# The weighted sums of graph layer 3: transposed one-hots of a whole group by one VectorE compare, one-hots on ScalarE, picks and scores a group ahead

## The reference

```
ft = (feat @ W.T).reshape(n, 4, 64)
a1 = einsum('nhd,hd->nh', ft, attn_l);  a2 = einsum('nhd,hd->nh', ft, attn_r)
e  = leaky_relu(a1[src] + a2[dst], 0.2)
m  = segment_max(e, dst)
ex = exp(e - m[dst])
s  = segment_sum(ex, dst)
out = elu(segment_sum(ft[src] * (ex / s[dst]), dst))
```

## Time and profile before

| | us |
|---|---|
| three runs | 6770.54, 6778.85, 6797.03 |
| span of the profiled execution | 6776.8 |
| of it the stage `L3Max` | 5426 to 6074 |
| of it the stage `L3Sum` | 6074 to 6476 |
| first and last exponential of `L3Sum` (51 groups apart) | 6085.5 and 6468.1 |

### The profile page before, as it was taken

The page is one execution under the profiler, slowest core; times in us unless marked ns, Lnnn a source line. Parts: engine busy times, 40 slices in busy tenths (PEclk is TensorE's granted clock), DMA queues, the critical chain, the costliest instruction groups (busy, mean ns, idle before and its releaser), DMA issues. The chain is left out here.

```text
span 6776.8 us, 96400 instructions
## 1 busy us (share of the span) xinstructions
PE 4712.7 (70%) x22485; PEld 3146.3 (46%) x22485; DVE 3844.5 (57%) x15258; ACT 2230.7 (33%) x8279; POOL 3457.0 (51%) x3739
## 2 busy tenths in 40 slices
PE   4566675748885555638667774888778478878858
PEld 3223333637772222424356663666567233336635
DVE  8676543120016666351567777777532667778876
ACT  0000001202232222302355554444323188874421
POOL 3646665546636666456555553555112166656610
PEclk9786656869995776855799997999879699989978
DMA  1133335546745666013154444777456156564410
GB/s 47 50 97 92 92 92 172 178 140 225 233 138 158 179 181 170 4 49 102 48 149 125 126 125 140 209 208 207 137 145 176 45 169 173 172 155 140 141 44 20
DMA packets 510322, 889.51 MB, mean 131 GB/s; under 512 B 97783, under 2 KB 380358, under 8 KB 501334
## 3 DMA queue, kind: packets, MB, share of 16 engines
q0 software_dynamic: 170800, 477.14, 25.9%
q1 hardware_dynamic: 278544, 277.57, 13.1%
q10 hardware_dynamic: 60438, 128.64, 6.1%
HBM read 711.86 MB, written 171.14 MB: 130 GB/s over the span
## 5 line engine op out<-in xcount | busy, mean ns | idle before, releaser
L998 PE MATMUL bank<-small 128*125 128x256 f32 x1660 | 760.6, 583 | 475.7 <-DVE small L965 269.5
L946 POOL DMA_INDIRECT small<-tabA,idxD x830 | 803.9, 969 | 449.0 <-issue 189.2
L998 PEld LDWEIGHTS bank<-small 128*125 128x125 f32 x1660 | 359.9, 265 | 875.7 <-issue 457.0
L977 DVE TENSOR_TENSOR big<-big,bank 125x256 f32 x830 | 347.6, 419 | 492.0 <-PE bank L998 308.1
L2467 POOL DMA_INDIRECT small<-tabC,idxD x415 | 394.2, 950 | 342.3 <-issue 123.2
L2509 ACT ACTIVATE small<-cst,small 128x128 f32<-128x128 f32 x1660 | 532.3, 388 | 95.8 <-issue 42.0
L2520 PE MATMUL bank<-small 128*125 128x512 f32 x830 | 474.2, 655 | 125.8 <-issue 97.5
L2221 POOL DMA_INDIRECT big<-tabB,idxD x415 | 392.1, 945 | 321.2 <-PE bank L2287 199.5
L1341 DVE COPY small<-bank 128x256 f32<-128x256 f32 x176 | 74.6, 425 | 832.3 <-PE bank L1381 405.5
L2026 POOL DMA_INDIRECT small<-tabT,idxS x415 | 392.3, 945 | 297.5 <-PE bank L1988 180.7
L780 POOL DMA_INDIRECT recs<-pkS,rowS x391 | 383.4, 981 | 256.1 <-issue 101.0
(11 more groups left out here) (460 smaller groups left out, 11594.9 us busy)
## 6 DMA issues: line engine op xcount, KB each, us to landing
small<-eaS SPq DMA_DIRECT2D x830, 128.0 KB
big<-in_L_w ACTq DMA_DIRECT2D x56, 1024.0 KB
eaS<-small SPq DMA_DIRECT2D x415, 128.0 KB
big<-in_L2f_w ACTq DMA_DIRECT2D x64, 512.0 KB
ytab<-small ACTq DMA_DIRECT2D x176, 128.0 KB
small<-tabA,idxD POOLq DMA_INDIRECT x830
idxS<-in_ea SPq DMA_DIRECT2D x78, 128.0 KB
locS<-in_ea SPq DMA_DIRECT2D x78, 128.0 KB
```

Source lines behind the costliest of these rows:

```text
L946: g.indirect_dma_start(out=self.gb[k % self.RG], out_offset=None, in_=K.tabA, in_offset=row_index(K.idxD, k)).then_inc(*self.got.up(k))
L977: v.tensor_tensor(rows, rows, K.bank[k % 4][0:PT, 0:D], ALU.add).then_inc(*self.added.up)
L998: p.matmul(self.K.bank[k % 4][0:PT, 0:D], self.oh[k % self.RO][:, 0:PT], self.gb[k % self.RG], start=True, stop=True).then_inc(*self.summe ...
```

## The change

Before `L3Max`'s own work, `LocRows` turns the table of local numbers: four transpositions on TensorE, four copies on ScalarE into bf16 rows, one DMA to the new DRAM table `rowsD`, and SP waits for it. `Flipped` then makes, in `L3Sum`, the 8 transposed one-hots of a group at once: SP reads 8 rows of `rowsD` into all 128 partitions (1024 bf16 each), and VectorE compares them with the partition's own number (`lane`). The transposition and the copy per tile are gone. The three parts are added by one reduction over PSUM. The one-hots are made on ScalarE, as relu(1 - (iota - loc)^2), two instructions, the second waiting for the first. Picks of group g+1 stand before the first product of group g, its scores after the third add of group g, its exponential after the sixth one-hot of group g. `RO` becomes 8, `RG` 16, and 6 PSUM banks hold products.

```diff
+class LocRows:
+    NB, P = 4, 104
+    def tensor(self, p):
+        for b in range(self.NB):
+            for c, (loc, table) in enumerate(self.pieces):
+                m = p.transpose(K.bank[4 + b][0:self.P, 128 * c:128 * c + 128], loc[:, self.P * b:self.P * (b + 1)], K.ident)
+        m.then_inc(*self.flipped.up)
+    def scalar(self, a):
+        a.wait_ge(*self.flipped.n(1))
+        for b in range(self.NB):
+            a.activation(self.row[0:self.P, w * b:w * (b + 1)], K.bank[4 + b][0:self.P, 0:w], ACT.Copy).then_inc(*self.turned.up)
+    def sync(self, s):
+        s.wait_ge(*self.turned.all)
+            s.dma_start(table.rearrange("(b p) e -> p b e", p=self.P), rows[:, :, c, :]).then_inc(*self.kept.up)
+        s.wait_ge(*self.kept.all)
+class Flipped:
+    G = 8
+    def sync(self, s, g):
+        if g >= 2:
+            s.wait_ge(*self.made.n(g - 1))
+        row = self.table[g * self.G:(g + 1) * self.G, :].rearrange("k e -> (k e)")
+        s.dma_start(self.row[g % 2], row.unsqueeze(0).broadcast_to([128, self.G * 128])).then_inc(*self.row_in.up(g))
+    def vector(self, v, g):
+        v.wait_ge(*self.row_in.n(g))
+        v.tensor_scalar(self.ohT[g % 2], self.row[g % 2], self.K.lane[:, 0:1], None, ALU.is_equal).then_inc(*self.made.up)
 class L3Max:
+        self.locs.sync(s)      # first in sync(); likewise locs.scalar(a), locs.tensor(p)
 class L3Sum:
-    GB, RO, RG = 8, 18, 8
+    GB, RO, RG, RS = 8, 8, 16, 6
     def sync(self, s):
+        self.flip.sync(s, 0)
+        self.flip.sync(s, 1)
         for k in range(NTE):
             if k >= self.RG:
                 s.wait_ge(*self.summed.n(k - self.RG + 1))
             s.dma_start(self.gb[k % self.RG][:, 0:D], K.eaS[k * 128:(k + 1) * 128, :]).then_inc(*self.got.up(k))
+            if k % self.GB == 0 and k // self.GB + 2 < self.n_g:
+                self.flip.sync(s, k // self.GB + 2)
+    def scores(self, v, gi):
+        v.wait_ge(*self.picked.n(gi + 1))
+        v.tensor_reduce(bv, b3, AXX, ALU.add).then_inc(*self.taken.up)
+        ...                                  # the four operations of lines 2609 to 2615
     def vector(self, v):
+        for k in range(NTE):
+            gi, j = k // self.GB, k % self.GB
+            if j == 1 and gi + 2 < self.n_g:
+                v.wait_ge(*self.picked.n(gi + 1))
+                flip.vector(v, gi + 2)
+            if j == 3 and gi + 1 < self.n_g:
+                self.scores(v, gi + 1)
+            rows = pr.acc[0:PT, bass.ds(at.at(k), AW)]
+            v.wait_ge(*self.summed.n(k + 1))
+            if k:
+                v.wait_ge(*self.added.n(k))
+            v.tensor_tensor(rows, rows, K.bank[2 + k % self.RS][0:PT, 0:AW], ALU.add).then_inc(*self.added.up)
+    def one_hot(self, a, k):
+        if k >= self.RO:
+            a.wait_ge(*self.summed.n(k - self.RO + 1))
+        a.activation(self.sq[k % 2], self.K.iota, ACT.Square, bias=self.negD[:, k:k + 1]).then_inc(*own.up)
+        a.wait_ge(*own.all)
+        a.activation(self.oh[k % self.RO], self.sq[k % 2], ACT.Relu, scale=-1.0, bias=self.K.ones[:, 0:1]).then_inc(*self.oneh.up)
     def scalar(self, a):
+        self.powers(a, 0)
+        for k in range(NTE):
+            self.one_hot(a, k)
+            if j == 5 and gi + 1 < self.n_g:
+                self.powers(a, gi + 1)       # waits for score(gi + 1), then Exp
+            if j == 0:
+                a.wait_ge(*self.expo.n(gi + 1))
+            if k >= self.RG:
+                a.wait_ge(*self.summed.n(k - self.RG + 1))
+            a.activation(self.gb[k % self.RG][:, D:AW], pr.EX[:, 4 * k:4 * k + 4], ACT.Copy).then_inc(*self.joined.up)
+    def pick(self, p, at, gi):
+        p.wait_ge(*self.flip.ready(gi * self.GB))
+        if gi >= 2:
+            p.wait_ge(*self.taken.n(gi - 1))
+        for j, k in enumerate(self.tiles(gi)):
+            m = p.matmul(K.bank[gi % 2][:, 24 * j:24 * j + 24], self.flip.at(k)[0:PT, :], pr.am3[0:PT, bass.ds(at.at(k), 24)], start=True, stop=True)
+        m.then_inc(*self.picked.up)
     def tensor(self, p):
+        self.pick(p, at, 0)
+        for k in range(NTE):
+            if k % self.GB == 0 and gi + 1 < self.n_g:
+                self.pick(p, at, gi + 1)
+            ...                              # waits for oneh, weighted, joined and added(k - 6), then the product
```

More of the change, by code:

```diff
@@ L1989, in split_sum, with __init__, at, ready @@
     return m
+class LocRows:
+    NB, P = 4, 104
+    def __init__(self, K, al, pieces):
+        self.K, self.pieces, self.n = K, pieces, len(pieces)
+        self.row = al(self.NB * self.n * 64, BF16)
+        self.flipped, self.turned, self.kept = K.mark(1), K.mark(self.NB), K.dma(self.n)
+    def tensor(self, p):
+        K = self.K
+        for b in range(self.NB):
[3 more added lines that the diff above has]
+    def scalar(self, a):
+        K, w = self.K, 128 * self.n
+        a.wait_ge(*self.flipped.n(1))
+        for b in range(self.NB):
+            a.activation(self.row[0:self.P, w * b:w * (b + 1)], K.bank[4 + b][0:self.P, 0:w], ACT.Copy).then_inc(*self.turned.up)
+    def sync(self, s):
+        rows = self.row[0:self.P, :].rearrange("p (b c e) -> p b c e", b=self.NB, c=self.n)
+        s.wait_ge(*self.turned.all)
+        for c, (loc, table) in enumerate(self.pieces):
+            s.dma_start(table.rearrange("(b p) e -> p b e", p=self.P), rows[:, :, c, :]).then_inc(*self.kept.up)
+        s.wait_ge(*self.kept.all)
+class Flipped:
+    G = 8
+    def __init__(self, K, table, al):
+        self.K, self.table = K, table
+        self.n_g = EP // self.G
+        self.row = [al(self.G * 64, BF16) for _ in range(2)]
+        self.ohT = [al(self.G * 64, BF16) for _ in range(2)]
+        self.row_in, self.made = K.ring(2, self.n_g), K.mark(self.n_g)
+    def sync(self, s, g):
[6 more added lines that the diff above has]
+        v.tensor_scalar(self.ohT[g % 2], self.row[g % 2], self.K.lane[:, 0:1], None, ALU.is_equal).then_inc(*self.made.up)
+    def at(self, k):
+        return self.ohT[k // self.G % 2][:, k % self.G * 128:(k % self.G + 1) * 128]
+    def ready(self, k):
+        return self.made.n(k // self.G + 1)
 class L2Max:
@@ L2457, in __init__ @@
         self.gb = [g(AW) for _ in range(self.RG)]
+        self.locs = LocRows(K, K.W, ((K.locD, K.rowsD),))
         self.got, self.kept_rows = K.ring(self.RG, NTE, "gather"), K.ring(self.RG, NTE)
@@ L2502, in scalar @@
         K, pr = self.K, self.pr
+        self.locs.scalar(a)
         for k in range(NTE):
@@ L2513, in tensor @@
         K, pr = self.K, self.pr
+        self.locs.tensor(p)
         for k in range(NTE):
@@ L2581, in gpsimd @@
             g.tensor_tensor(rows, rows, self.pr.EX[:, 4 * k:4 * k + 4].unsqueeze(2).broadcast_to([128, 4, 64]), ALU.mult).then_inc(*self.weighted.up)
+    def scores(self, v, gi):
+        K, pr, own = self.K, self.pr, self.K.own_v
+        c0, n = gi * self.GB, len(self.tiles(gi))
+        b3 = K.bank[gi % 2][:, 0:24 * n].rearrange("p (k c h) -> p k h c", c=3, h=8)
+        bv = self.ame[gi % 2][:, 0:8 * n].rearrange("p (k h) -> p k h", h=8)
+        A1v = pr.A1[:, 4 * c0:4 * (c0 + n)].rearrange("p (k h) -> p k h", h=4)
+        q = self.am4[gi % 2][:, 0:4 * n]
+        qv = q.rearrange("p (k h) -> p k h", h=4)
+        v.wait_ge(*self.picked.n(gi + 1))
+        v.tensor_reduce(bv, b3, AXX, ALU.add).then_inc(*self.taken.up)
+        v.wait_ge(*self.taken.n(gi + 1))
+        if gi >= 2:
+            v.wait_ge(*self.expo.n(gi - 1))
+        v.tensor_tensor(qv, A1v, bv[:, :, 0:4], ALU.add).then_inc(*own.up)
+        v.wait_ge(*own.all)
+        v.scalar_tensor_tensor(out=q, in0=q, scalar=0.2, in1=q, op0=ALU.mult, op1=ALU.max).then_inc(*own.up)
+        v.wait_ge(*own.all)
+        v.tensor_tensor(qv, qv, bv[:, :, 4:8], ALU.subtract).then_inc(*own.up)
+        v.wait_ge(*own.all)
+        v.tensor_scalar(q, q, 0.0, None, ALU.min).then_inc(*self.score.up)
@@ L2623, in vector @@
[L2623 to L2643 removed]
+        flip.vector(v, 0)
@@ new lines, in vector @@
+        flip.vector(v, 1)
+        self.scores(v, 0)
+        for k in range(NTE):
[10 more added lines that the diff above has]
+            v.tensor_tensor(rows, rows, K.bank[2 + k % self.RS][0:PT, 0:AW], ALU.add).then_inc(*self.added.up)
@@ new lines, in vector, with powers @@
+        v.wait_ge(*self.added.all)
+    def one_hot(self, a, k):
+        if k >= self.RO:
+            a.wait_ge(*self.summed.n(k - self.RO + 1))
+        own = self.K.own_a
+        a.activation(self.sq[k % 2], self.K.iota, ACT.Square, bias=self.negD[:, k:k + 1]).then_inc(*own.up)
+        a.wait_ge(*own.all)
+        a.activation(self.oh[k % self.RO], self.sq[k % 2], ACT.Relu, scale=-1.0, bias=self.K.ones[:, 0:1]).then_inc(*self.oneh.up)
+    def powers(self, a, gi):
+        t = self.tiles(gi)
+        a.wait_ge(*self.score.n(gi + 1))
+        a.activation(self.pr.EX[:, 4 * t[0]:4 * t[-1] + 4], self.am4[gi % 2][:, 0:4 * len(t)], ACT.Exp).then_inc(*self.expo.up)
```

113 lines of the change are left out of this document (27 added, 86 removed).

## The result

The changed kernel takes 6834.82 us (median of 4 runs, 6827.31 to 6842.22), the kernel before, in four runs (the three above and one more), 6785.74. The ratio is 1.0072, 95% interval 1.0052 to 1.0091: slower, by 49 us. A second comparison, on a chip on which the kernel before takes 5981.15 us, gave 6030.82, ratio 1.0086 [1.0067, 1.0105]. The other stages are faster there; `L3Sum` is not. The forecast was 6805, the range 6757 to 6842.

A forecast was written before the change was run, and what follows sets the result against it. VectorE set the old 7.50 us beat; the changed round trip averages 7.6, plus 0.33 for the clock and 0.07 for stretched compares, 8.0 us per group: +26 us, 6805 on the median, range 6757 to 6842.

The forecast's parts named there:

- The forecast's case: In `L3Sum`, a period between 7.5 and 8.6 us per group of 8 tiles, 6779 to 6835 us; chance 0.48.
- ScalarE: In `L3Sum`, ScalarE's work takes 0.88 us a tile and 7.17 a group, a floor under the period.
- The last product of the group before: On TensorE, it starts at 0.05 us, when its one-hot is ready, and keeps TensorE for 0.51.
- Picks: On TensorE, eight picks before product 0 take 0.80 us; product 0 starts at 1.36 instead of 0.92.
- Load of offsets: On TensorE, ahead of every second block of picks: costs 1.1 to 1.2 us, covers the product's 0.51; period 7.95.
- Compare: On VectorE, the compare of 1024 16-bit columns takes 0.43 us, from 2.60 to 3.03, ahead of the second add.
- Rival C: In `L3Sum`, the compare meets GpSimd's multiplications and is 0.47 us late in every group: +50 us, 6829; chance 0.12.
- Clock: TensorE's granted clock in `L3Sum` is 0.87, a quarter of the time at 1.2 GHz, costing 0.33 us per group.
- Sum: Over `L3Sum`'s 51 intervals, 8.0 us against 7.50 gives 25.5, plus 0.5, less 0.2 for the tail: +26 us.
- A: In `L3Sum`, buffers hide VectorE's and TensorE's delays and ScalarE's 7.17 us sets the beat: -15 us, 6763; chance 0.20.
- B: In `L3Sum`, TensorE's lower clock holds all through, period 8.9 us: +71 us, 6850; chance 0.12.
- D: In `L3Sum`, ScalarE takes some 0.6 us a tile and VectorE's work sets 6.8: -36 us, 6743; chance 0.08.

## Why the prediction was right, and where not

The time fell into the range, near its upper end and 30 us above the number given; 7 of the 30 are the kernel before, whose fourth run raised its median, 23 are the change. The forecast's case occurred, in its upper part: the period of 8.33 is above the 8.17 from which a difference can be told, so the outcome is slower, which had 0.39, and not within 0.5%, which had 0.53. The mechanism was right in the main: every second period is longer, the exponential waits for the last score in all 52 groups, and the clock costs what was said. Sizes were off, all in the round trip, and one limit was overlooked.

*ScalarE.* 0.82 us per tile, not 0.88. The relu follows 0.42 after the square, not 0.49: its wait for ScalarE's own result costs 0.03 where the earlier trace rows showed 0.10. By its own words the prediction would be wrong in this term, and was, but towards a lower floor (6.8 instead of 7.17), which the loop never let show. From the exponential to the next group's first square go 1.88, not 1.99. With the loop cut ScalarE is the floor (the version with load early and exponential late).

*The last product of the group before.* I let it start when its one-hot was ready, at 0.05. It also waits for the small copy behind the relu, and starts at 0.31. Put ahead of the one-hot, the copy gave 0.21 per group back.

*Picks.* 0.80 forecast, 1.06 from the first pick to product 0 (6309.60 to 6310.66). The product ahead of them is in their way for 0.32 only, not 0.51. Together product 0 starts at 1.69, not 1.36. The exponential comes at 5.54 instead of 5.27, and the period is 7.42 instead of 7.26.

*Load of offsets, the step that failed most.* I let it begin with the last product and end 1.2 later, picks at 1.25. It takes 1.11, but it stands behind both weight loads of that product, so the first pick comes 1.51 after the product and not 1.20. A group with a load is 0.65 longer than forecast at full clock, 8.60 for 7.95: 0.26 by the copy, 0.31 by the load, 0.29 by the picks behind it, less 0.21 in small terms (0.84 instead of 0.90 from product 0 to its add, where by the earlier trace rows I should have added 0.92, and ScalarE's shorter tiles). On the mean that is 0.33, nearly the whole error. That the load mattered at all was right, and its early version shows it: without it at the group's edge the change costs nothing.

*Compare.* 0.43 forecast, 0.48 measured. Rival C did not decide the time, but the reason given against it is only half right. GpSimd's multiplications do end about as the compare starts, but in a group without a load slightly later: the compare is held to 5.26 after the exponential in 12 of 49 groups and lasts 0.51 to 0.55 there, under 0.02 per group on the mean where I had put 0.07. What the prediction doesn't have is that this makes a limit of its own, 7.42, right behind the loop that I added up. The runs with early picks, with the small copy ahead and, in part, with the exponential late ran into it; there its price was up to 0.50 (0.98 long), and 0.36 with the one-hots on VectorE, where I had 0.47.

*Clock.* 0.87 and 0.33 per group forecast, 0.87 and 0.33 measured. The agreement is luck: I took a clock between those of other stages and put it to the missing transpositions. The run with the load early has these missing too and a clock of 0.99. It is the load at the group's edge that lets it fall, so both costs have one cause.

*Sum.* 7.6 + 0.33 + 0.07 = 8.0 forecast, 8.0 + 0.33 = 8.33 measured. Of the 0.33 missed, 0.33 lie in the groups with a load and 0.08 in the others, and the 0.07 for stretched compares did not come. 51 x 0.33 = 17 of the 23 us missed on the profiled execution. The tail was 1.4 us longer, not 0.2 shorter, since its products wait for one-hots 0.82 apart, and 4.3 came from other stages. `LocRows` cost nothing: from the first gather to the last reduction `L3Max` takes 646.5 us in both kernels. A, B and D did not occur. The early load comes near A's number (7.42), but not to its cause, since the exponential still waits in all 52 groups.

## What to carry to other kernels

When a change turns two independent streams into a loop over three engines, add up the loop at its joints: what each engine has queued ahead of and behind the waiting instruction, small copies included. Add up a second loop for each engine that the same result sets off, and see what runs at the same time as it: here GpSimd's multiplications, which hold up a compare that has nothing to do with them. Several runs that end at one and the same period (7.42) are the sign of such a limit. A load of offsets belongs into the slack of a group, not at its edge, and an instruction that waits for a far result behind all that others need now. Both are moves of a line, and took this change from 0.9% slower to 0.6% faster than before.

## What the runs showed of the hardware

- A load of 16 offsets takes 1.11 us in TensorE's queue and 1.10 in VectorE's (26 of each in the changed kernel). On TensorE it starts behind both weight loads of the product ahead of it, 0.25 after that product's start, and the next weight load comes 1.51 after it; the product's multiplication runs on beside the load (until 6165.97, the load being at 6165.5). On VectorE the load puts 0.75 us between two adds.
- One such load per 16 tiles, at the edge of a group, goes with a granted clock of 0.87 in the stage, and of 0.99 when it is moved into slack; the slow stretch can fall into the next group (0.78, behind a group at 1.00). Such a load is not the only thing that does this: with the one-hots on VectorE the stage is at 0.91 although the load is in slack.
- A wait of ScalarE for its own last result cost 0.03 us between 128-column operations, 0.10 in the earlier trace rows.
- One-hots of 0.28 us between dependent adds are free on VectorE: adds stay 0.62 apart with them (6311.30, 6311.92 and 6312.55 in the kernel before) and without.
- The wide compare takes 0.48 us alone. When it runs beside GpSimd's multiplications it is held: over eleven of the kernels all 336 compares longer than 0.49 us end 0.28 or 0.29 after the end of a multiplication. The length depends on the phase: in the run with the exponential late, compares that start 4.26 to 4.28 us after the exponential take 0.48, and GpSimd's last multiplication ends later (5.21 to 5.23); those that start at 4.29 to 4.41 take 0.85 to 0.98.
